# Loading Wk in float32 on SyncE's queue with casts on ScalarE, and moving two evictions from VectorE to ScalarE

## The reference

```python
mod = silu(c) @ wmod                       # six vectors: sa, ca, ga, sb, cb, gb
ga, gb = sign(.) * max(abs(.), 0.25)
h = layernorm(x) * (1 + ca) + sa
q, k = relu(h Wq^T) / 8, relu(h Wk^T) / 8  # 16 heads of 64
v, u = h Wv^T, silu(h Wu^T)
kv = k^T v                                 # per head, over all 2048 tokens
x = x + ga * ((rmsnorm(q kv) * u) Wo^T)
h = layernorm(x) * (1 + cb) + sb
x = x + gb * (int8-style quantised h times int8-style quantised weight^T + bias)
```

## Time and profile before

| | us |
|---|---|
| median of 3 runs | 467.24 (465.77 to 469.17) |
| the profiled execution | 464.44 |
| its span on core 7, the slowest | 462.9 |
| span of the other cores | 457.6 to 461.5 |
| busy: TensorE, VectorE, ScalarE, POOL | 393.4, 278.2, 230.2, 91.9 |
| mean granted TensorE clock, both dies | 0.959 |

### The profile page before, as it was taken

How to read it: one execution, slowest core, us unless ns; L and a number is a source line. 1 busy time by engine, 2 the same in 40 slices (tenths; PEclk the granted TensorE clock), 3 DMA queues, 4 the chain that set the end, 5 groups by cost and what they waited for, 6 DMA issues and landing times.

```text
span 462.9 us, 6418 instructions; the slowest of 8 cores (457.6 to 462.9 us)
## 1 busy us (share of the span) xinstructions
PE 393.4 (85%) x2054; PEld 185.1 (40%) x2054; DVE 278.2 (60%) x494; ACT 230.2 (50%) x328; POOL 91.9 (20%) x148
## 2 busy tenths in 40 slices
PE   3042659999999998969888899999999999999964
PEld 1020234455445444324334344444444444444431
DVE  3455662464872537488455776457655775668883
ACT  3341233466267332667456853586743766434340
POOL 2321411230361101000020211212121221222220
PEclk9995689999999999999899999999999999999997
DMA  7999899789986999996999407644755375465986
GB/s 195 269 272 299 243 200 238 246 250 312 317 314 152 263 237 277 220 293 233 342 225 273 114 1 136 93 86 96 137 92 96 86 138 91 80 108 93 149 125 129
DMA packets 19618, 87.05 MB, mean 188 GB/s; under 512 B 2681, under 2 KB 2689, under 8 KB 14722
## 3 DMA queue, kind: packets, MB, share of 16 engines
q0 software_dynamic: 8544, 31.49, 38.5%
q1 hardware_dynamic: 11042, 55.16, 37.5%
HBM read 70.36 MB, written 24.67 MB: 205 GB/s over the span
## 4 chain that ended last, share of the span: by engine, by line
PE 34%; DMA 26%; DVE 17%; issue 9%; ACT 7%; SPq 3%; POOL 2%; DVEq 0%; ACTq 0%; POOLq 0%
PE pb L359 30%; DMA stage<-wmod_b 10%; DMA wa<-wmod_a 8%; DMA xr<-x_tm 7%; DVE stage L426 4%; SPq L44 3%; DVE h L766 2%; DVE am L769 2%; ACT rn L680 2%; DVE wm_c L482 1%; DVE bn L300 1%; ACT rn L683 1%; DMA row_g<-rows 1%; PE pb L788 1%; PE pb L668 1%
## 5 line engine op out<-in xcount | busy, mean ns | idle before, releaser
L359 PE MATMUL pb<-h,wu_s 128*128 128x512 bf16 x256 | 61.8, 385 | 1.2 <-ACT u_s L657 1.2
L359 PE MATMUL pb<-fq,xqT 128*128 128x512 bf16 x256 | 61.4, 385 | 0.9 <-ACT xqT L792 0.9
L359 PE MATMUL pb<-h,wq_s 128*128 128x512 bf16 x256 | 61.4, 384 | 0.0
L359 PE MATMUL pb<-wo_s,u_s 128*128 128x512 bf16 x256 | 60.5, 382 | 1.0 <-DVE u_s L660 1.0
L359 PE MATMUL pb<-wv_s,h 128*128 128x512 bf16 x256 | 58.4, 379 | 0.0
L426 DVE SCALAR_TENSOR_TENSOR stage<-stage,silr 128x1024 f32<-128x1024 f32 x32 | 37.7, 1219 | 21.9 <-DMA stage<-wmod_b 21.9
L359 PE MATMUL pb<-wk_s,h 128*128 128x512 bf16 x208 | 45.7, 379 | 0.0
L685 DVE SCALAR_TENSOR_TENSOR q_s<-rn,pb 128x512 bf16<-128x512 f32 x32 | 22.0, 686 | 30.0 <-ACT rn L683 29.5
L359 PEld LDWEIGHTS pb<-wo_s,u_s 128*128 128x128 bf16 x256 | 25.2, 99 | 31.7 <-issue 2.8
L359 PEld LDWEIGHTS pb<-h,wu_s 128*128 128x128 bf16 x256 | 24.8, 99 | 30.6 <-issue 3.9
L359 PEld LDWEIGHTS pb<-h,wq_s 128*128 128x128 bf16 x256 | 25.0, 98 | 29.4 <-issue 1.0
(11 more groups left out here) (105 smaller groups left out, 563.3 us busy)
## 6 DMA issues: line engine op xcount, KB each, us to landing
stage<-wmod_b SPq DMA_DIRECT2D x16, 1024.0 KB, 12.2
xr<-x_tm SPq DMA_DIRECT2D x21, 512.0 KB, 3.5
wa<-wmod_a SPq DMA_DIRECT2D x8, 1024.0 KB, 34.4
out_tm<-row_gbb SPq DMA_DIRECT2D x4, 2048.0 KB, 19.4
out_tm<-xr POOLq DMA_DIRECT2D x15, 512.0 KB, 8.2
out_tm<-h POOLq DMA_DIRECT2D x15, 512.0 KB, 6.3
xr<-x_tm POOLq DMA_DIRECT2D x8, 512.0 KB, 16.8
stage<-wo SPq DMA_DIRECT2D x4, 1024.0 KB, 6.0
```

The costliest lines, as they stand in the source:

```text
L359: t = PE.do(lambda e, dc=dc: e.matmul(pb[bank][:], lhs(dc), rhs(dc), start=(dc == 0), stop=(dc == NC - 1)), *after, each(dc) if each else ...
```

## The change

Wk's pieces are loaded as float32 into `wkf` by SyncE, in one queue with x and wmod's pieces: `before` says which pieces of Wk come ahead of which piece of wmod. ScalarE casts each into `wk`, in the opening's step of the same number. `wkf[0..3]` lie where `row_g` to `row_gbb` will be, `wkf[4..7]` where `wv` will be. So Wv's first half and the first `get` wait for the cast of piece 7 as well. The second edit: of tile 1's evictions only those of c = 3 stay with VectorE, and those of c = 1 go to ScalarE.

```diff
+    wkf = [sb(f"wkf{dc}", [128, D], at=(rows_at if dc < 4 else wv_at - 16384) + 4096 * dc)
+           for dc in range(NC)]
...
     def load_wk(dc):
-        w_tok["wk", dc] = POOL.dma(sl_k8[dc], wk[:, dc], bass.AP(d_w["wk"], dc * D, [[NC * D, 128], [1, D]]))
+        wkf_tok[dc] = SP.dma(sl_k8[dc], wkf[dc][:], bass.AP(d_w["wk"], dc * D, [[NC * D, 128], [1, D]]))
+
+    def cast_wk(dc):
+        w_tok["wk", dc] = ACT.do(lambda e: e.copy(out=wk[:, dc], in_=wkf[dc][:]), wkf_tok[dc])
...
     first = {0: (0, 1), 1: (2, 3), 2: (4, 5), 3: (6,), 4: (7,)}
+    before = {1: (0, 1), 2: (2, 3), 3: (4,), 4: (5,), 5: (6,), 6: (7,)}
     for dc in range(NC):
         for g in first.get(dc, ()):
             load_x(SP, g, g, ())
+        for c in before.get(dc, ()):
+            load_wk(c)
         wa_tok[dc] = SP.dma(sl_a[dc], wa[dc][:],
...
-            if i == 1 and c % 2:
+            if i == 1 and c == 3:
                 ev_tok[i, dc] = DVE.do(lambda e, d=d, dc=dc: e.tensor_scalar(
...
             stats(g)
             xhat(g)
-            load_wk(g)
         if dc == 1:
             for c in range(4):
                 transp(0, c)
+        for c in before.get(dc, ()):
+            cast_wk(c)
         wa_sum(dc)
...
-    load_w("wv", wv, 0, wa_tok[6])
+    load_w("wv", wv, 0, wa_tok[6], w_tok["wk", NC - 1])
...
         if n == 3:
-            row(0, row_g)
+            row(0, row_g, w_tok["wk", NC - 1])
```

More of the change, by code:

```diff
@@ L120, in build_nc @@
     silr = sb("silr", [128, D])
+    rows_at = cur[0]
     row_g = sb("row_g", [128, D])
@@ L230, in load_wk @@
     def load_wk(dc):
-        w_tok["wk", dc] = POOL.dma(sl_k8[dc], wk[:, dc], bass.AP(d_w["wk"], dc * D, [[NC * D, 128], [1, D]]))
+        wkf_tok[dc] = SP.dma(sl_k8[dc], wkf[dc][:], bass.AP(d_w["wk"], dc * D, [[NC * D, 128], [1, D]]))
+    def cast_wk(dc):
+        w_tok["wk", dc] = ACT.do(lambda e: e.copy(out=wk[:, dc], in_=wkf[dc][:]), wkf_tok[dc])
+    wkf_tok = {}
     def load_w(w, dst, hf, *after):
```

## The result

The changed kernel takes 471.85 us (median of 4 runs, 470.9 to 473.79) against 467.33 before: a ratio of 1.010 with an interval of 1.0051 to 1.015, so 4.5 us slower. Run again later beside other kernels it took 471.55 against 466.92, ratio 1.009 (1.0058 to 1.0123). In some executions of every kernel the cores of one die run at a lower granted clock and take longer (522.61 us in one of e1's, clock 0.81); medians and ratios here leave those out. The forecast was 470.7, with the change slower, in a range of 466 to 473. The profiled execution took 472.16 us; its slowest core is core 4, span 470.6.

The account below looks back on a forecast made before the run. Bound: the load chain through Wv's issue, x's group 11 and VectorE's wmod_b sums to kv_bd. Delay +4.0 less 0.5 gives +3.5: 467.9 us for the profiled execution, 470.7 for the median; range 466.0 to 473.0.

Parts of the forecast that it names:

- (4): Wv's first half waits for cast 7, so POOL issues it at 59.5 us instead of 55.53, 4.0 us later.
- term (1): Wk's load on SyncE's queue instead of POOL's casting queue: 12.7 us of all engines instead of 14.5, saving 1.8 us.
- Term (2): Loads land in order of issue on one queue: wmod_a's piece 5 at 49.2 us instead of 52.5.
- (3): ScalarE's casts, 1.24 us each; cast 7 behind tile 1's evictions, so 10.3 us from piece 5's landing to Wv's issue.
- (5): Second edit starts TensorE's dense stretch 2.5 to 4 us earlier; lost again at kvprod(0, 2) and transp(3, 0).
- worse: Rival: piece 5 lands at 50.5 us or later, TensorE's waits lower its clock, late loads collide; +6, 473.2 us; chance 0.10.
- faster: Rival: the float32 queue runs at 364 GB/s, Wv is issued 2.2 us earlier than before; 465.0 us; chance 0.13.
- slack: Rival: the wait at kv_bd or DMA's pause from 90 to 98 us absorbs the delay; +0 to +1.5, 468.0 us; chance 0.15.

Follow-up runs that it names:

- e1: The changed kernel with the second edit undone, VectorE evicting c = 1 of tile 1 again: 469.20 us, ratio 1.004 to before.
- e4: The kernel before with one added wait: Wv's first half also waits for the evictions of transp(1, 1): 469.77 us, ratio 1.0061.
- e12: The changed kernel with wkf4 to wkf7 in kT's and vT's place, Wv not waiting for casts, Wk's piece 7 loaded behind wmod's piece 6: 466.40 us, ratio 0.9997.
- e2: The changed kernel with the casts of Wk's pieces 6 and 7 ahead of all tile 1 evictions on ScalarE: 468.73 us, ratio 1.0039 to before.
- e3: The kernel before with the second edit alone, Wk still cast by POOL's queue: 467.09 us, ratio 0.9994.
- e8: The kernel before with the second edit and x's groups 10 and 11 loaded ahead of Wv's second half: 460.78 us, ratio 0.9866.
- e5: The changed kernel with wkf4 to wkf7 in kT's and vT's place and Wv's first half waiting only for wmod's piece 5: 467.27 us, ratio 1.001.

## Why the prediction was right, and where not

**The mechanism (4) was right.** It was forecast that cast 7 would stand behind tile 1's evictions, that POOL would issue Wv near 59.5 us, that DMA would run dry until about 62 us and that all behind it would shift. Measured on core 4: 60.44 us, a share of 0.03 from 58 to 62, group 11's statistics at 93.89 us instead of 92.0, kv_bd at 188.89 instead of 185.7. Over the cores the issue is 4.5 us later than before, where 4.0 was forecast, and the time 4.5, where 3.5 was. The profiled execution, forecast at 467.9 us, took 472.16: the medians lie closer to the forecast than the two profiles do. e4 reproduces most of the loss by one wait; e12 removes it.

**The saving of 1.8 us in term (1) was wrong.** The rates of the two queues, 329 and 290 GB/s as read, were taken for prices of the two kinds of load. From 25 to 40 us SyncE's queue alone now moved this:

```profile
q1 hardware_dynamic: 1033, 4.86, 99.9%
```

4.86 MB were read in those 15 us. Before it was 3.25 MB and twice 0.79 MB (the casting queue's figure is what it wrote): 4.83 MB; over all eight cores the means are 4.91 MB now and 4.93 before. The bytes read per us are the same, so the load neither gains nor loses by its queue. The rule that the prediction weighed and put aside, that reading binds (the Trainium skill, DMA: Bandwidth & Descriptors, "Where 436 GB/s comes from"), is the one that held here; the rate itself, 324 GB/s, lies under the page's figure of about 358.

**Term (2), wa5's landing, came 2.6 us too late for it**: 51.8 us instead of 49.2, of which 1.8 is the saving that wasn't there. **The sum behind it in (3) was too long**, by about the same: 8.6 us (51.89 to 60.44) instead of 10.3. The cast takes 1.04 us and not xhat's 1.24, and k_step(5) ran at the full clock, 1.49 us instead of 2.72: TensorE had been busy without a gap from 51.07 to 54.65 us at 0.50, and the granted clock was 1.00 from 56 us on. The two errors, +2.6 and -1.7 us, cancel in the issue; that it came within a us of the forecast is luck.

**A part of the delay was not seen.** wa6 was put at 53 to 54.5 us. It landed at 56.7 (core 4; at 55.0 on core 7 before), because all of Wk stands ahead of it. Over the eight cores VectorE takes it up from its landing at 55.2 to 57.2 us, 56.2 on average, 3.6 us before the mean issue of Wv (0.5 us on core 7 before). e2 measured the order at 1.8 us (0.5 to 3.2) of the 4.5: even with the casts out of the way, it alone is slower. The DMA engines therefore ran dry from 58 us and not from 55.

**The wait was taken as given, and it is wider than the buffers ask.** Prediction and change have Wv's first half wait for cast 7 because wkf4 to wkf7 lie in wv_s. By the addresses in the kernel only wkf4 and wkf5 lie where the first half goes; wkf6 and wkf7 lie in the second half's place. Cast 5 had ended at 52.4 us on core 4, before piece 6 landed. A first half that waits for cast 5 and a second half that waits for cast 7 would have taken the casts off this path with no other place for wkf; no run tried it.

**(5), TensorE's gain and its double loss, was right in kind.** Start at 64.2 to 66.3 us (forecast 64 to 65.5); new wait for ScalarE at kvprod(0, 2), 4.99 us; kvprod(0, 2) 2.1 us later than before instead of at the same time, since nmr(11) was ready at 100.2 us and not at 98.3; the wait at transp(3, 0) ends at 142.88 us, 4.8 later, where 3.5 was forecast. Of the rival *worse* a part is in the result: the granted clock did fall to 0.50 at that first wait, on cores 1, 2, 4 and 7. The rivals *faster* and *slack* fell. The first asked for 364 GB/s and the queue gave 324; the cores that had slack before lost it, kv_bd waits for TensorE on none, and DMA's pause before 98 us was still there (share 0.01 from 95 to 97 us on core 4).

**What stays open:** why e4's 4.0 us of delay cost 2.9 us and the change's own delay its full size. The fall of the clock is one candidate: from 90 to 108 us the granted clock stays at 1.00 on all eight cores in e4, and falls to 0.50 on four in the change and on six when it ran again. Against it stands that kv_bd waits for TensorE on no core of the change. Noise is the other candidate, since the intervals overlap.

## What to carry to other kernels

Before a cast, copy or eviction is put on an idle engine, look at what stands in front of it in that engine's order and at what waits for it: here each of the eight casts takes 1 us of an idle engine, and the last one held a load back by some 3 us on core 4, while 16 DMA engines ran nearly empty. A buffer that is borrowed from the next load's target turns the borrower's last reader into that load's releaser; another place (e12) took the wait away. And check which part of the load each borrowed piece really lies under. Where two chains end together, a gain on one is worth nothing by itself (e3: 0.3 us) and a loss on either counts (e4: 2.9 of 4.0 us); shorten both (e8) or none.

## What the runs showed that was not expected

The two ends of the first pass are balanced within 2 us: with Wv issued 2.6 us earlier (e5, with the float32 load) the bound is TensorE, 4 us later (e4) VectorE's chain, and the time is not below that of before in either case.

Cores come in pairs of unlike speed. e3's cores:

```profile
core 0: 464.8 us, clock 0.956
core 1: 456.3 us, clock 0.964
core 2: 464.6 us, clock 0.963
core 3: 456.1 us, clock 0.962
core 4: 456.0 us, clock 0.981
core 5: 464.2 us, clock 0.963
core 6: 461.3 us, clock 0.967
core 7: 456.4 us, clock 0.964
```

In each pair 0-1, 2-3, 4-5, 6-7 one core is 5 to 9 us behind the other; which one it is changes from run to run, and in some runs a pair is nearly even. In this execution the core that is behind moved fewer bytes from 60 to 85 us (245 and 273 GB/s on cores 0 and 1, 231 and 272, 244 and 260, 251 and 277 in the other pairs, the slower core first) and its group 11 is taken up later (88.5 and 85.1 us on cores 0 and 1). So the slowest core here is one that got the smaller share, and a chain of loads is worth more in the metric than a mean over the cores shows. That the two cores of a pair share an HBM stack is what the Trainium skill says (HBM Reference, "Specifications (TRN2)"); no run here varied it. In e8 all spans lie within 4 us (454.6 to 458.5); the chain of waits of its slowest core no longer goes through group 11, but through TensorE from 65.5 to 125 us.
